# A two-block conditioned transformer on one core: x normalised on ScalarE in attention, attention's stages reordered, and setup cut at another place

## The chip, the cores and the metric

One core of one Trainium2 chip runs one program. The metric is its device time in microseconds (us), the median of several executions. The engines are named as in the profile: PE is TensorE's matmul and PEld its weight load, DVE VectorE, ACT ScalarE, POOL GpSimd, SP SyncE. A name with a q (SPq, ACTq) is the engine's queue, which issues DMAs.

## What is computed

x is (128, 64, 256) in f32: 128 sequences of 64 rows and 256 channels; cond is (128, 256), one row per sequence. The first block, cut to its core:

```
ada = silu(cond) @ ada_w.T + ada_b        # 6 rows of 256 per sequence: gamma1,2 scale1,2 shift1,2
x1  = ln(x) * (scale1 + 1) + shift1
q, k, v = split(x1 @ mat_qkv_w.T + bias)  # 16 heads of 16
q = l2norm(q) * exp(scale_mul);  k = l2norm(k)
o   = softmax(q @ k.T) @ v
x   = x + (o @ proj_w.T + proj_b) * gamma1
x2  = ln(x) * (scale2 + 1) + shift2
x   = x + (gelu(x2 @ fc1_w.T + fc1_b) @ fc2_w.T + fc2_b) * gamma2
```

The second block is linear attention with a modulation of its own, `silu(cond) @ emb_W + emb_b` (the third modulation here), and a last product.

## The kernel before

The program has four parts, each a block of instructions for all engines, with a barrier of all engines between them: setup (L187), attention_pass (L444), feed_forward_pass and linear_pass. x stays in SBUF as x_all, 64 tiles of two sequences (128 rows) in 16 groups of four. The change touches setup and attention_pass.

*Setup.* SyncE's queue loads cond, proj_w, ada_w (1.5 MB), the first group of x (512 KB), the qkv weights (768 KB) and emb_w (512 KB), waits for the gammas, stores them to DRAM and loads three more groups of x. PE multiplies the activated cond: first with the gamma columns (512 wide, L349), then 16 products with 2*C and more (scale and shift 1 and 2, L354), then 8 for the third modulation (L361). VectorE adds the biases (L398 to L418). Every f32 weight is split in a high and a low bf16 half: ScalarE makes the high one (L289, L291), POOL subtracts (L322, L324).

*Attention.* Five engines run the tiles as a software pipeline. Each engine has a list of stages with a lag: at step n it does, in the list's order, each stage of tile n - lag. So the order in the list is the order of the instructions on that engine, and everything across engines is a semaphore wait. The first 16 steps are written out, the middle is a loop over four steps, the last steps are written out again. `reuse(eng, sem, t, slots)` waits until a buffer of `slots` copies is free.

```
pipeline(sp, [(9, load_gain), (5, place_v), (5, place_k), (0, load_later)])
pipeline(pool, [(5, normalise), (1, rstd_of), (12, add), (2, x1_low), (8, e_lo), (0, split_fc)])
```

A tile goes so: statistics and aggregate on DVE (mean, variance), rstd_of on POOL, hat on DVE (L916: x_hat = (x - mean) * rstd, 128x256), turn_x on PE (two transposes into ps_x), modulate on DVE and modulate_second on ACT (x1_t), x1_high on ACT and x1_low on POOL (x_split), qkv on PE (six products of 512 columns into ps_qk, L809, and six of 256 into ps_v, L816), biases on DVE, v_hi on ACT and v_low on DVE, square on ACT, reduce_norms on DVE (L837, L839), logs and factor on ACT, normalise on POOL (qk_hat, L630), turn_qk on PE (L800), qk_hi on ACT (L710), qk_lo on DVE (L908). place_v and place_k on SyncE copy v and k into block form inside SBUF, for two tiles at a time: at odd tiles, four DMAs into v_pairs (L608) and eight into k_pairs (L593). place_v waits for pv_done of the tile four before, which frees the buffer; place_k for qk_lo. Then scores on PE (48 small products, L790, waits for the eight k copies), high_exponentials and full_exponentials on ACT (L725, L730), e_lo on POOL (L657, 128x1024), probs_v on PE (L775, signals pv_done), outputs on DVE, turn_o on PE (L764), o_hi on ACT, o_low on DVE, project on PE (L751, L754), residual on DVE, add on POOL. ps_y of project and ps_v of qkv share a bank, as do ps_x's halves for turn_x and turn_o; bank_free waits keep them apart. load_gain loads the rows of gamma1 from DRAM for two tiles. load_later loads the other 12 groups of x and the fc weights; split_fc splits these at tiles 7 and 14 (ACT) and one later (POOL, 128x2048).

Of the kernel before, what the change touches and what calls it, by code (L numbers as in the profile page):

```python
# [109 lines left out]


class Shared:


    def __init__(self, nc, ctx):
# [5 lines left out]
        self.minus_half = sb("minus_half", [P, UNROLL], F32)  # L121
        self.eps_norm3 = sb("eps_norm3", [P, 1], F32)
# [64 lines left out]
def setup(nc, m, x, cond, qkv_w, q_bias, scale_mul, proj_w, proj_b, ada_w, ada_b, fc2_b,  # L187
          emb_w, out_b, columns):

    with ExitStack() as ctx:  # L190
# [8 lines left out]
        cond_t = sb("cond_t", [P, NC_, B])  # L199
        w_ada = sb("w_ada", [P, NC_, 6 * C])  # L200
        w_emb = sb("w_emb", [P, NC_, 2 * C])
        b_ada_row = sb("b_ada_row", [P, 2 * C])
        b_ada, b_emb, g_sn, b_sn = m.b_ada, m.b_emb, m.g_sn, m.b_sn
        gamma_rows = sb("gamma_rows", [P, 2 * C])
# [3 lines left out]
        scale_plus = sb("scale_plus", [P, NC_, B])  # L208
        b_sn_half = sb("b_sn_half", [P, NC_])
# [8 lines left out]
        ps = [ctx.enter_context(nc.psum_tensor(f"set_ps{i}", [P, 512], F32)) for i in range(6)]  # L218
# [4 lines left out]
        emb_here = sem("emb_here")  # L223
# [14 lines left out]
        b_halved = sem("b_halved")  # L238
# [5 lines left out]
        modulations = sem("modulations")  # L244
        gammas_made = sem("gammas_made")
        gammas_stored = sem("gammas_stored")
# [10 lines left out]
        def _(sp):  # L257
            load(sp, [(cond_sb[:], cond)], cond_here)
            load(sp, [(proj_full[:], proj_w.rearrange(CHUNKED, p=P))], proj_here)
            load(sp, [(w_ada[:], ada_w.rearrange(CHUNKED, p=P))], ada_here)  # L260
            load(sp, [(m.x_all[:, X_PARTS[0]:X_PARTS[1]], x_tiles(x)[:, X_PARTS[0]:X_PARTS[1]])], m.x_here[0])
            load(sp, [(qkv_full[:], qkv_w.rearrange(CHUNKED, p=P))], qkv_here)
            load(sp, [(w_emb[:], emb_w.rearrange(CHUNKED, p=P))], emb_here)
            sp.wait_ge(gammas_made, 1)
            sp.dma_start(m.gammas, gamma_rows[:]).then_inc(gammas_stored, 16)
            sp.wait_ge(gammas_stored, 16)
            part = slice(X_PARTS[1], X_PARTS[2])
            load(sp, [(m.x_all[:, part], x_tiles(x)[:, part])], m.x_here[1])
            sp.wait_ge(attention_here, 16)

        @block.scalar
        def _(act):
# [8 lines left out]
            load(act, [(m.b_fc2[:], row(fc2_b))], m.ff_here)  # L281
# [5 lines left out]
            act.activation(m.norm_weight[:, 0:H], head_scale[:], ACT.Exp, scale=-2.0)  # L287
            act.wait_ge(qkv_here, 16)
            act.activation(m.w_qkv[:, HI], qkv_full[:], ACT.Copy).then_inc(qkv_hi_made, 1)  # L289
            act.wait_ge(proj_here, 16)  # L290
            act.activation(m.w_proj[:, HI], proj_full[:], ACT.Copy).then_inc(proj_hi_made, 1)  # L291

        @block.gpsimd
        def _(pool):
# [6 lines left out]
            pool.memset(m.eps_ln[:], 1e-6).then_inc(consts_made, 1)  # L301
            pool.memset(m.same_head[:], 1.0).then_inc(consts_made, 1)
# [16 lines left out]
            pool.memset(m.v_split[:, :, :, HI, :, 2 * HD:], 1.0)  # L319
            pool.wait_ge(rows_cleared, 2)  # L320
            pool.wait_ge(qkv_hi_made, 1)
            pool.tensor_tensor(m.w_qkv[:, LO], qkv_full[:], m.w_qkv[:, HI], ALU.subtract)  # L322
            pool.wait_ge(proj_hi_made, 1)
# [1472 lines left out]
```

## Time and profile before

| | us |
|---|---|
| median of 3 runs | 1266.47 |
| lowest, highest | 1264.91, 1266.75 |
| the profiled execution, its own time | 1262.96 |
| its span, first to last instruction | 1261.2 |
| setup | 0 to 24.5 |
| attention | 24.5 to about 495 |

| engine | busy us | share |
|---|---|---|
| PE | 1128.5 | 89% |
| PEld | 818.5 | 65% |
| DVE | 960.6 | 76% |
| ACT | 795.3 | 63% |
| POOL | 848.9 | 67% |

Busy time counts neither waits nor the issue of DMAs. The shares are means over parts with different limits, so the order of work in attention has to be read from timelines. In a timeline, several instructions of a group are drawn together (x48), and the bracket at the end gives the idle time of the engine before the first of them, and what released it. TensorE's loads of weights (PEld) start with their products and overlap them.

### The profile page before, as it was taken

The page shows a single profiled execution, that of the slowest core. Times are in us where ns is not written, and L with a number is a line of the kernel's source. Part 1 is how long each engine was busy: PE and PEld are TensorE (multiplying, and loading weights), DVE is VectorE, ACT ScalarE, POOL GpSimd, SP SyncE. Part 2 cuts the span into 40 slices and gives each one's busy share as a digit, 9 for nine tenths or more (in the row PEclk, how much of TensorE's full clock was granted, in tenths as well). Part 3 has the DMA queues.
Part 4 walks back from the last instruction along what each step waited for, and adds up shares of the span by engine and source line. Part 5 has one row for each costly group of instructions (what it writes and reads, how often), then busy time and mean ns, then how long its engine had stood idle before and what let it go on. Part 6 is the DMA issues. An engine that isn't in the chain of part 4 may idle for free. (4 is left out here: it accounts for less than half of the span.)

```text
span 1261.2 us, 37486 instructions
## 1 busy us (share of the span) xinstructions
PE 1128.5 (89%) x11946; PEld 818.5 (65%) x12098; DVE 960.6 (76%) x2338; ACT 795.3 (63%) x2141; POOL 848.9 (67%) x1018
## 2 busy tenths in 40 slices
PE   4687999999999975699999999997899999999997
PEld 3476677777777764366666676765566666766664
DVE  6687999999999963755655555543899999999985
ACT  2676787887787862445544545441677777777774
POOL 4667777777777754537675667563367777777777
PEclk9898999999999998699999999998999999999999
DMA  7552222222222221200101010100011111111112
GB/s 265 145 147 52 63 55 60 61 57 59 62 57 59 62 54 32 76 18 18 34 17 33 17 33 17 34 18 17 6 28 56 42 40 56 42 54 42 39 57 81
DMA packets 138945, 68.13 MB, mean 54 GB/s; under 512 B 76544, under 2 KB 137600, under 8 KB 138880
## 3 DMA queue, kind: packets, MB, share of 16 engines
q1 hardware_dynamic: 110480, 41.32, 13.1%
q10 hardware_dynamic: 28400, 25.99, 7.2%
q8 instruction: 35, 0.57, 0.2%
q14 instruction: 30, 0.25, 0.1%
HBM read 41.58 MB, written 8.65 MB: 40 GB/s over the span
## 5 line engine op out<-in xcount | busy, mean ns | idle before, releaser
L1128 PE MATMUL f_ps_y<-w_fc,f_h_split 128*128 128x256 bf16 x1536 | 172.7, 273 | 1.4 <-DVE f_branch L1247 1.4
L1155 PE MATMUL f_ps_h<-f_x_split,w_fc 128*128 128x512 bf16 x737 | 166.4, 383 | 4.3 <-DVE f_biases L1278 1.4
L1128 PEld LDWEIGHTS f_ps_y<-w_fc,f_h_split 128*128 128x128 bf16 x1536 | 150.2, 98 | 22.5 <-issue 1.7
L657 POOL TENSOR_TENSOR e_split<-e_full,e_split 128x1024 bf16<-128x1024 f32 x64 | 136.5, 2133 | 39.7 <-ACT e_full L730 39.7
L1255 DVE TENSOR_TENSOR f_h_split<-f_h,f_h_split 128x512 bf16<-128x512 f32 x64 | 64.0, 1002 | 104.3 <-ACT f_h L1114 104.2
L1489 ACT ACTIVATE l_z_t<-l_ps_yt,shift,scale 128x64 f32<-128x64 f32 x256 | 82.6, 402 | 92.3 <-PE l_ps_yt L1555 56.2
L1155 PEld LDWEIGHTS f_ps_h<-f_x_split,w_fc 128*128 128x128 bf16 x768 | 75.6, 99 | 88.7 <-issue 3.3
L1113 ACT ACTIVATE f_h_split<-f_ps_h,columns 128x512 bf16<-128x512 f32 x128 | 89.1, 696 | 66.5 <-POOL f_h_split L1074 36.2
L790 PE MATMUL ps_s<-qk_t,k_pairs 128*128 128x64 bf16 x3072 | 102.6, 195 | 29.0 <-DMA k_pairs<-qk_t 25.4
L790 PEld LDWEIGHTS ps_s<-qk_t,k_pairs 128*128 128x128 bf16 x3072 | 97.9, 99 | 37.3 <-issue 19.0
L1074 POOL TENSOR_TENSOR f_h_split<-f_h,f_h_split 128x512 bf16<-128x512 f32 x64 | 79.7, 1255 | 36.6 <-ACT f_h L1114 36.6
L637 POOL TENSOR_TENSOR x_split<-x_t,x_split 128x256 bf16<-128x256 f32 x64 | 42.9, 671 | 84.0 <-ACT x_split L678 84.0
L1606 PE MATMUL l_ps_qv<-w_qvk,l_x_split 128*128 128x512 bf16 x324 | 82.3, 383 | 13.9 <-issue 6.6
L1101 ACT ACTIVATE f_x_split<-f_x 128x1024 bf16<-128x1024 f32 x16 | 16.9, 1057 | 118.9 <-POOL f_x L1041 118.9
L1114 ACT ACTIVATE f_h<-f_ps_h,columns 128x512 f32<-128x512 f32 x128 | 89.6, 700 | 0.0
L809 PE MATMUL ps_qk<-w_qkv,x_split 128*128 128x512 bf16 x323 | 83.3, 390 | 4.3 <-POOL x_split L637 0.8
L725 ACT ACTIVATE e_split<-ps_s,minus_shift 128x1024 bf16<-128x1024 f32 x64 | 71.2, 1112 | 21.2 <-PE ps_s L790 21.1
L1458 POOL TENSOR_TENSOR l_rstd<-l_mean_var,eps_norm 128x2 f32<-128x2 f32 (+1 forms) x73 | 14.1, 194 | 101.5 <-DVE l_mean_var L1649 76.2
L1520 ACT ACTIVATE l_kq<-l_ps_k,l_k_tops 128x64 f32<-128x64 f32 x256 | 77.9, 341 | 1.1 <-DVE l_k_tops L1684 0.9
L730 ACT ACTIVATE e_full<-ps_s,minus_shift 128x1024 f32<-128x1024 f32 x64 | 70.8, 1106 | 0.0
L630 POOL TENSOR_TENSOR qk_hat<-qk,factors 128x512 f32<-128x512 f32 x64 | 67.7, 1058 | 1.5 <-ACT factors L703 1.5
L1041 POOL TENSOR_TENSOR f_x<-f_x,shift 128x1024 f32<-128x1024 f32 x16 | 31.0, 1940 | 53.7 <-DVE f_x L1187 53.7
(180 smaller groups left out, 3152.5 us busy)
## 6 DMA issues: line engine op xcount, KB each, us to landing
v_pairs<-v_split SPq DMA_DIRECT2D x128, 66.0 KB, 2.1
k_pairs<-qk_t SPq DMA_DIRECT2D x256, 32.0 KB, 2.2
gain<-gammas SPq DMA_DIRECT2D x64, 128.0 KB, 3.1
f_gain<-gammas ACTq DMA_DIRECT2D x32, 256.0 KB, 4.3
l_gate<-in_cond ACTq DMA_DIRECT2D x128, 64.0 KB, 2.6
out<-x_all ACTq DMA_DIRECT2D x16, 512.0 KB, 2.9
x_all<-in_x SPq DMA_DIRECT2D x13, 512.0 KB, 5.6
fc_full<-in_L_cond_fc_w SPq DMA_DIRECT2D x2, 1024.0 KB, 7.5
```

What stands on the lines that cost most here:

```text
L657: pool.tensor_tensor(flat(e_split[a][:, LO]), flat(e_full[:]), flat(e_split[a][:, HI]), ALU.subtract).then_inc(e_lo_made, 1)
L725: act.activation(flat(e_split[a][:, HI]), flat(ps_s[:]), ACT.Exp, bias=m.minus_shift[:])
L790: last = pe.matmul(ps_s[:, s, G_ * c + g], k_pairs[:, t.slot(4), k, c, s, g].rearrange("p r k -> p (r k)"), qk_t[:, 0, t.slot(4), q, c, s ...
L809: last = pe.matmul(ps_qk[:, :], x1_split[a][:, xs, c, :], m.w_qkv[:, ws, c, 0:2 * C], start=(i == 0 and c == 0), stop=(i == 2 and c == NC_ ...
L1074: pool.tensor_tensor(h_split[a][:, LO, f], h[f % 4][:], h_split[a][:, HI, f], ALU.subtract).then_inc(h_lo_odd, 1)
L1113: act.activation(h_split[a][:, HI, f], ps_h[f % 4][:], ACT.Gelu, bias=m.b_fc1[:, f:f + 1])
L1114: act.activation(h[f % 4][:], ps_h[f % 4][:], ACT.Gelu, bias=m.b_fc1[:, f:f + 1]).then_inc(h_made, 1)
L1128: last = pe.matmul(ps_y[:, i], h_split[a][:, hs, f, i * P:(i + 1) * P], m.w_fc2[:, ws, f], start=(f == 0 and k == 0), stop=(f == F_CHUNKS ...
L1155: last = pe.matmul(ps_h[f % 4][:], m.w_fc1[:, ws, c, f * P:(f + 1) * P], x2_split[a][:, xs, c], start=(k == 0 and c == 0), stop=(k == 2 an ...
L1489: act.activation(z_t[a][:, c, s * L:(s + 1) * L], ps_yt[:, c, s * L:(s + 1) * L], ACT.Identity, bias=by_seq(m.shift3, c, t, s), scale=by_s ...
L1520: act.activation(kq[t.slot(4)][:, i * L:(i + 1) * L], ps_k[:, c, s * L:(s + 1) * L], ACT.Exp, bias=k_tops[a][:, c, s:s + 1], scale=-1.0, a ...
L1606: last = pe.matmul(ps_qv[:], x3_split[a][:, xs, c], m.w_qvk3[:, ws, c, 0:2 * C], start=(i == 0 and c == 0), stop=(i == 2 and c == NC_ - 1))
```

## The change

In attention:

- The five lists are reordered, as below. hat moves from DVE to ACT and becomes an activation with scale rstd and bias centre = -mean * rstd; POOL makes centre in two more operations on 128x1, each behind a wait. statistics keeps its lag, rstd_of goes from lag 1 to 0, hat from 1 to 0, normalise on POOL from 5 to 4, place_v and place_k from 5 to 6.
- load_gain's wait for branch_made now also stands in the loop.
- The third modulation's products are made by PE in step 0 (into ps_s), its eight VectorE operations in steps 1 and 2 (four each, the last in the list). The first scores wait for them, as does SyncE's load of the fc1 weights at tile 3, since the tiles they use now lie in that buffer. fc2_b is loaded by SyncE in step 0.

In setup:

- SyncE loads the qkv weights ahead of x, and the three later groups of x before it waits for the gammas; it no longer waits for their store.
- PE makes the 16 products for scales and shifts first, then the gammas.
- k_pairs is cleared by VectorE for three quarters, later in its order, and by POOL for one. ACT splits proj_w first, then the qkv weights. VectorE, not POOL, makes the low half of proj_w. POOL's low half of the qkv weights comes last.

```diff
             load(sp, [(w_ada[:], ada_w.rearrange(CHUNKED, p=P))], ada_here)
+            load(sp, [(qkv_full[:], qkv_w.rearrange(CHUNKED, p=P))], qkv_here)
             load(sp, [(m.x_all[:, X_PARTS[0]:X_PARTS[1]], x_tiles(x)[:, X_PARTS[0]:X_PARTS[1]])], m.x_here[0])
-            load(sp, [(qkv_full[:], qkv_w.rearrange(CHUNKED, p=P))], qkv_here)
-            load(sp, [(w_emb[:], emb_w.rearrange(CHUNKED, p=P))], emb_here)
-            sp.wait_ge(gammas_made, 1)
-            sp.dma_start(m.gammas, gamma_rows[:]).then_inc(gammas_stored, 16)
-            sp.wait_ge(gammas_stored, 16)
+            load(sp, [(m.w_emb, emb_w.rearrange(CHUNKED, p=P))], m.emb_here)
             part = slice(X_PARTS[1], X_PARTS[2])
             load(sp, [(m.x_all[:, part], x_tiles(x)[:, part])], m.x_here[1])
+            sp.wait_ge(gammas_made, 1)
+            sp.dma_start(m.gammas, m.gamma_rows).then_inc(m.gammas_stored, 16)
...
+            pool.memset(m.k_pairs[:, 3], 0.0)
...
-            pool.tensor_tensor(m.w_proj[:, LO], proj_full[:], m.w_proj[:, HI], ALU.subtract)
...
+            dve.tensor_tensor(m.w_proj[:, LO], proj_full[:], m.w_proj[:, HI], ALU.subtract)
...
             def load_gain(t):
-                if isinstance(t.n, int):
-                    reuse(sp, branch_made, t, 4)
+                reuse(sp, branch_made, t, 4)
...
                 if isinstance(t.n, int) and t.n == FC1_AT:
+                    sp.wait_ge(m.gammas_stored, 16)
+                    sp.wait_ge(modulations3_made, NC_)
...
-            pipeline(sp, [(9, load_gain), (5, place_v), (5, place_k), (0, load_later)])
+            pipeline(sp, [(6, place_v), (6, place_k), (0, load_later), (9, load_gain)])
...
+                pool.wait_ge(rstd_made, t.n + 1)
+                pool.tensor_tensor(centre[t.slot(4)][:], mean_var[t.slot(4)][:, 0:1], rstd[t.slot(4)][:], ALU.mult
+                                   ).then_inc(mean_scaled, 1)
+                pool.wait_ge(mean_scaled, t.n + 1)
+                pool.tensor_tensor(centre[t.slot(4)][:], centre[t.slot(4)][:], m.minus_one[:], ALU.mult
+                                   ).then_inc(centre_made, 1)
...
-            pipeline(pool, [(5, normalise), (1, rstd_of), (12, add), (2, x1_low), (8, e_lo), (0, split_fc)])
+            pipeline(pool, [(12, add), (0, split_fc), (0, rstd_of), (2, x1_low), (8, e_lo), (4, normalise)])
...
+            def hat(t):
+                a = t.slot(2)
+                act.wait_ge(centre_made, t.n + 1)
+                reuse(act, x_hat_t, t, 2)
+                act.activation(x_hat[a][:, None, :], t.rows(m.x_all), ACT.Identity, bias=centre[t.slot(4)][:],
+                               scale=rstd[t.slot(4)][:]).then_inc(x_hat_made, 1)
...
-            pipeline(act, [(4, v_hi), (4, square), (2, modulate_second), (8, high_exponentials), (5, qk_hi),
-                           (10, o_hi), (2, x1_high), (8, full_exponentials), (4, logs), (0, split_fc),
-                           (4, factor)])
+            pipeline(act, [(2, modulate_second), (4, v_hi), (4, square), (2, x1_high), (8, high_exponentials),
+                           (10, o_hi), (4, logs), (5, qk_hi), (8, full_exponentials), (4, factor), (0, split_fc),
+                           (0, hat)])
...
+            def emb_products(t):
...
             def scores(t):
                 a = t.slot(2)
+                if isinstance(t.n, int) and t.n == 0:
+                    pe.wait_ge(modulations3_made, NC_)
...
-            pipeline(pe, [(8, scores), (11, project), (5, turn_qk), (9, probs_v), (10, turn_o), (3, qkv), (1, turn_x)])
+            pipeline(pe, [(8, scores), (9, probs_v), (10, turn_o), (5, turn_qk), (11, project), (1, turn_x),
+                          (3, qkv), (0, emb_products)])
...
+            def modulation3(t):
...
-            pipeline(dve, [(4, biases), (2, modulate), (4, v_low), (10, outputs), (4, reduce_norms),
-                           (11, residual), (10, o_low), (1, hat), (5, qk_lo), (-1, statistics), (0, aggregate)])
+            pipeline(dve, [(2, modulate), (4, biases), (10, outputs), (-1, statistics), (4, v_low), (0, aggregate),
+                           (4, reduce_norms), (10, o_low), (5, qk_lo), (11, residual), (0, modulation3)])
```

What this makes of PE's order in one step of attention, before, from the scores (ps_s) to turn_x:

```order
L790 MATMUL ps_s<-qk_t,k_pairs 128x64 x48
L751 MATMUL ps_v<-bias_rows,ones 128x256
L754 MATMUL ps_v<-w_proj,o_t 128x256 x6
L800 MATMUL ps_qkt<-ident,qk_hat 128x128 x4
L775 MATMUL ps_o<-v_pairs,e_split 128x66 x24
L764 MATMUL ps_x<-ident,o_full 128x128 x2
L809 MATMUL ps_qk<-w_qkv,x_split 128x512 x6
L816 MATMUL ps_v<-w_qkv,x_split 128x256 x6
L826 MATMUL ps_x<-ident,x_hat 128x128 x2
```

and the same step of PE with the change:

```order
L803 MATMUL ps_s<-qk_t,k_pairs 128x64 x48
L776 MATMUL ps_o<-v_pairs,e_split 128x66 x24
L765 MATMUL ps_x<-ident,o_full 128x128 x2
L813 MATMUL ps_qkt<-ident,qk_hat 128x128 x4
L752 MATMUL ps_v<-bias_rows,ones 128x256
L755 MATMUL ps_v<-w_proj,o_t 128x256 x6
L839 MATMUL ps_x<-ident,x_hat 128x128 x2
L822 MATMUL ps_qk<-w_qkv,x_split 128x512 x6
L829 MATMUL ps_v<-w_qkv,x_split 128x256 x6
```

probs_v (ps_o) and turn_o stand directly behind the scores; project went from second to behind turn_qk, and turn_x ahead of qkv.

ACT's order in one step, before, with the semaphores that each waits for:

```order
L690 ACTIVATE v_split<-ps_v 128x2x4x32 [waits v_pairs_here0,qkv_done]
L684 ACTIVATE squares<-qk 128x512 [waits norms_made,qk_biased]
L670 ACTIVATE x_t<-ps_x,shift,scale 128x64 [waits x1_lo_made,x1_made]
L670 ACTIVATE x_t<-ps_x,shift,scale 128x64
L725 ACTIVATE e_split<-ps_s,minus_shift 128x1024 [waits pv_done,scores_done]
L710 ACTIVATE qk_t<-ps_qkt 128x2x256 [waits scores_done,qk_turned]
L736 ACTIVATE o_t<-ps_x 128x256 [waits proj_done,o_turned]
L678 ACTIVATE x_split<-x_t 128x256 [waits qkv_done,x1_second]
L730 ACTIVATE e_full<-ps_s,minus_shift 128x1024 [waits e_lo_made]
L696 ACTIVATE log_norms<-norms 128x32 [waits factors_made,norms_weighted]
L703 ACTIVATE factors<-log_norms,log 128x32 [waits qk_hat_made,logs_made]
```

and with the change:

```order
L664 ACTIVATE x_t<-ps_x,shift,scale 128x64 [waits x1_lo_made,x1_made]
L664 ACTIVATE x_t<-ps_x,shift,scale 128x64
L691 ACTIVATE v_split<-ps_v 128x2x4x32 [waits v_pairs_here0,qkv_done]
L685 ACTIVATE squares<-qk 128x512 [waits norms_made,qk_biased]
L679 ACTIVATE x_split<-x_t 128x256 [waits qkv_done,x1_second]
L726 ACTIVATE e_split<-ps_s,minus_shift 128x1024 [waits pv_done,scores_done]
L737 ACTIVATE o_t<-ps_x 128x256 [waits proj_done,o_turned]
L697 ACTIVATE log_norms<-norms 128x32 [waits factors_made,norms_weighted]
L711 ACTIVATE qk_t<-ps_qkt 128x2x256 [waits scores_done,qk_turned]
L731 ACTIVATE e_full<-ps_s,minus_shift 128x1024 [waits e_lo_made]
L704 ACTIVATE factors<-log_norms,log 128x32 [waits qk_hat_made,logs_made]
L672 ACTIVATE x_hat<-x_all,centre,rstd 128x256 [waits x_hat_t,centre_made]
```

x1_high (x_split) now comes ahead of the high exponentials, logs ahead of qk_hi and of the full exponentials, and x_hat stands last.

## Rows read from the trace of the kernel before

**Rows 1.** Attention, one stretch: busy us of PE, PEld, DVE, ACT, POOL; clock, DMA share
```profile
180.00:240.00 60.00, 55.61 (x871) 42.73 (x878) 56.02 (x134) 47.74 (x99) 46.34 (x54) 1.00 0.27 59
```

**Rows 2.** Timeline of PEld, one pair of steps: start, us, line, tiles
```profile
209.77 1.46 PEld L790 LDWEIGHTS ps_s<-qk_t,k_pairs 128*128 128x128 bf16 x48 [0.49 <-issue]
211.40 0.10 PEld L751 LDWEIGHTS ps_v<-bias_rows,ones 128*128 128x128 bf16 x1 [0.17 <-issue]
...
212.16 0.42 PEld L800 LDWEIGHTS ps_qkt<-ident,qk_hat 128*128 128x128 f32 x4
212.55 0.89 PEld L775 LDWEIGHTS ps_o<-v_pairs,e_split 128*128 128x128 bf16 x24
...
213.54 1.07 PEld L809 LDWEIGHTS ps_qk<-w_qkv,x_split 128*128 128x128 bf16 x6
...
215.74 0.20 PEld L826 LDWEIGHTS ps_x<-ident,x_hat 128*128 128x128 f32 x2 [0.26 <-issue]
215.91 1.55 PEld L790 LDWEIGHTS ps_s<-qk_t,k_pairs 128*128 128x128 bf16 x48
...
223.18 0.40 PEld L790 LDWEIGHTS ps_s<-qk_t,k_pairs 128*128 128x128 bf16 x12 [0.66 <-issue]
```

**Rows 3.** SyncE's queue beside it, and its wait for probs_v in the whole run
```profile
213.59 2.60 SPq L608 DMA_DIRECT2D v_pairs<-v_split  x4
216.32 5.24 SPq L593 DMA_DIRECT2D k_pairs<-qk_t  x8
...
SPq L608 <- PE ps_o L775: 90.8, 24, 8.4
```

**Rows 4.** Waits from 60 to 450 us: in total, times, longest
```profile
PE ps_s L790 <- DMA k_pairs<-qk_t: 12.5, 26, 1.6
```

**Rows 5.** Groups from 60 to 450 us: busy us, mean ns, idle before
```profile
L916 DVE TENSOR_SCALAR x_hat<-x_all,mean_var,rstd 128x256 f32 (+1 forms) x56 | 46.8, 836 | 5.8 <-POOL rstd L624 5.8
...
L670 ACT ACTIVATE x_t<-ps_x,shift,scale 128x64 f32<-128x64 f32 x112 | 39.1, 399 | 1.4 <-DVE x_t L849 0.2
...
L839 DVE SCALAR_TENSOR_TENSOR norms<-norms,norm_weight 128x32 f32<-128x32 f32 x56 | 31.0, 553 | 1.9
...
L678 ACT ACTIVATE x_split<-x_t 128x256 bf16<-128x256 f32 x57 | 23.2, 408 | 0.0
...
L622 POOL TENSOR_TENSOR rstd<-mean_var,eps_ln 128x1 f32<-128x1 f32 x56 | 10.7, 191 | 0.0
```

**Rows 6.** The tile ps_s in the whole run; ACT and POOL in that pair
```profile
L790 PE MATMUL ps_s<-qk_t,k_pairs x3072: 189/193/242, 51.0 to 489.9; 128*128 128x64 bf16 x192
...
212.94 0.60 ACT L710 ACTIVATE qk_t<-ps_qkt 128x512 bf16<-128x512 f32 x1
...
214.44 1.11 ACT L730 ACTIVATE e_full<-ps_s,minus_shift 128x1024 f32<-128x1024 f32 x1
...
215.62 2.13 POOL L657 TENSOR_TENSOR e_split<-e_full,e_split 128x1024 bf16<-128x1024 f32 x1 [0.25 <-ACT e_full L730]
```

**Rows 7.** Setup and the first tiles: the first 35 us, and rows of the timeline
```profile
0.00:35.00 35.00, 17.11 (x77) 11.53 (x79) 22.05 (x49) 9.54 (x16) 16.05 (x34) 0.86 0.82 277
...
11.87 3.50 PE L349 MATMUL set_ps<-w_ada,cond_t 128*128 128x512 f32 x4
...
15.21 3.73 PE L354 MATMUL set_ps<-cond_t,w_ada 128*128 128x128 f32 x32
...
16.28 1.48 ACT L289 ACTIVATE w_qkv<-qkv_full 128x1536 bf16<-128x1536 f32 x1 [5.89 <-DMA qkv_full<-in_L_cond_mat_qkv_w]
...
22.08 0.34 DVE L410 TENSOR_SCALAR scale_plus<-set_ps,columns 128x128 f32<-128x128 f32 x1
...
24.54 0.89 DVE L895 BATCH_NORM_STATS2 stats<-x_all 128x6 f32<-128x256 f32 x2 [0.30 <-PEq L190]
...
26.44 0.41 DVE L916 TENSOR_SCALAR x_hat<-x_all,mean_var,rstd 128x256 f32<-128x256 f32 x1 [0.94 <-POOL rstd L624]
...
36.26 0.19 DVE L839 SCALAR_TENSOR_TENSOR norms<-norms,norm_weight 128x32 f32<-128x32 f32 x1
```

More of the change, by code:

```diff
@@ L346, in _ @@
             pe.wait_ge(ada_here, 16 * 2)
-            for c in range(NC_):
-                last = pe.matmul(ps[1][:, :], cond_t[:, c, :], w_ada[:, c, 0:2 * C], start=(c == 0), stop=(c == NC_ - 1))
-            last.then_inc(products, 1)
             for k in range(8):
@@ L357, in _ @@
             last.then_inc(products, 1)
-            pe.wait_ge(emb_here, 16)
-            for k in range(4):
-                for c in range(NC_):
-                    last = pe.matmul(ps[4][:, k * B:(k + 1) * B], w_emb[:, c, k * P:(k + 1) * P], cond_t[:, c, :],
-                                     start=(c == 0), stop=(c == NC_ - 1))
+            for c in range(NC_):
+                last = pe.matmul(ps[1][:, :], cond_t[:, c, :], w_ada[:, c, 0:2 * C], start=(c == 0), stop=(c == NC_ - 1))
             last.then_inc(products, 1)
@@ L780, in probs_v @@
                 last.then_inc(pv_done, 1)
+            def emb_products(t):
+                if isinstance(t.n, int) and t.n == EMB_AT:
+                    pe.wait_ge(m.emb_here, 16)
+                    for k in range(4):
+                        for c in range(NC_):
+                            last = pe.matmul(flat(ps_s[:])[:, k * B:(k + 1) * B], m.w_emb[:, c, k * P:(k + 1) * P],
+                                             m.cond_t[:, c, :], start=(c == 0), stop=(c == NC_ - 1))
+                    last.then_inc(emb_done, 1)
             def scores(t):
                 a = t.slot(2)
+                if isinstance(t.n, int) and t.n == 0:
+                    pe.wait_ge(modulations3_made, NC_)
                 pe.wait_ge(k_pairs_here[t.u // 2], (t.j + 1) * 16 * HPC)
@@ L910, in qk_lo @@
                                   qk_t[:, :, t.slot(4), HI].rearrange("p w c k -> p w (c k)"), ALU.subtract).then_inc(qk_lo_made, 1)
-            def hat(t):
-                a = t.slot(2)
-                dve.wait_ge(rstd_made, t.n + 1)
-                reuse(dve, x_hat_t, t, 2)
-                dve.tensor_scalar(x_hat[a][:, None, :], t.rows(m.x_all), mean_var[t.slot(4)][:, 0:1], rstd[t.slot(4)][:],
-                                  ALU.subtract, ALU.mult).then_inc(x_hat_made, 1)
             def biases(t):
```

93 lines of the change are left out of this document (50 added, 43 removed).

## The prediction

> **What bounds the kernel now.** I read the busy times of one stretch of the attention loop first, then the timeline of TensorE's weight loads, since it shows where the stages of a tile begin, then SyncE's queue beside it, and the waits last. From 180 to 240 us PE is busy 55.6 of 60 us and DVE 56.0 [rows 1]; both look like the bound, and neither is it alone. The starts of the scores tell more: 209.77, 215.91, 223.18 [rows 2]. The steps alternate, 6.14 and 7.27 us, and only the pair, 13.41, repeats. At the end of the long step PE waits for the DMA of k_pairs: 26 such waits in the 57 tiles from 60 to 450 us [rows 4], one in nearly every pair. SyncE copies k and v of two tiles at a time, in order on one queue. At 213.59, right behind probs_v of that step (its loads begin at 212.55), it issues four copies of v, at 216.32 eight copies of k, and the scores that need them begin at 223.18 [rows 2, 3]. SyncE's waits for that product sum to 90.8 us [rows 3], so it is the product that releases it. The ring is: scores to v 3.82, v to k 2.73, k to the next scores 6.86; 13.41 in all, exactly the pair. While this ring stands, less work on any engine gives nothing. In its first leg PE does project (from 211.40) and turn_qk (from 212.16) between the scores and probs_v [rows 2].
>
> **What stands next under it.** 60 us hold 8.95 tiles of 6.705. Busy per tile: DVE 6.26, ACT 5.33, POOL 5.18, PE 6.21 [rows 1]. PE's ends overlap its next starts. Taken from start to start, without waits, its stages need 1.46 for the scores, 0.76 project, 0.39 turn_qk, 0.99 probs_v with turn_o, 1.94 qkv (2.20 less the 0.26 idle), 0.17 turn_x: 5.71 [rows 2].
>
> **The change, part by part.**
>
> *PE's order.* probs_v and turn_o now stand directly behind the scores. The leg from scores to v becomes 1.46 + 1.04 (212.55 to 213.59) = 2.50 instead of 3.82 [rows 2, 3]. The ring is 2.50 + 2.73 + 6.86 = 12.09, or 6.05 a tile. This has two conditions. First, probs_v must find the low half of e_split. I lay out one step from the start of its scores, with durations from [rows 5, 6]: scores done 1.6, high exponential until 2.75 (as long as the full one), o_hi until 3.2 (turn_o ends near 2.7), logs until 3.35, qk_hi until 3.9, full exponential until 5.0 (1.11), POOL's low half until 7.2 (2.13). The next probs_v comes 1.46 behind the next scores, at 7.65 with 6.2 a tile: 0.45 to spare. Before, the full exponential began 4.67 behind the scores (214.44 against 209.77) [rows 2, 6], now at 3.9, because x1_high is done ahead of it. Second, k must be ready when v has been issued, at 5.2; qk_lo follows qk_hi and ends near 4.7: 0.5 to spare.
>
> *SyncE's order.* place_v and place_k move one step later in the list, gain behind them; but this queue is paced by its waits, and the sequence is still v, k, gain. v and k take 2.60 + 5.24 = 7.84 us of a pair [rows 3], so there is room for gain's two copies in 12. Their new wait is for branch_made of a tile whose residual comes right behind the qk_lo that k waited for, so it has passed before k's 5.24 us of issue are over. Cost nothing; if that residual came 5 us late, v and the ring would be late with it. The load of fc2 now goes ahead of a k, once.
>
> *x_hat to ScalarE.* VectorE loses 0.84 a tile [rows 5] and comes to 5.42. ScalarE gains one activation of 128x256 f32 out of SBUF. It has no such row; the nearest is x_split's 0.41, the far end two of x_t's 0.40 with scale and bias, 0.80 [rows 5]. I take 0.41, nearest in size: ScalarE 5.74. POOL gets two operations on 128x1 like rstd's first, 0.19 [rows 5], each with a handover of 0.08: 0.54 in all, POOL 5.72. POOL is idle 13.7 of 60 us now, 1.5 a tile [rows 1], which covers it; without that cover x_split's low half and the exponentials' would come 0.5 later. The chain to x_hat is longer by 0.54, but rstd_of and hat run a step ahead of turn_x, with about 3 us to spare. The Trainium skill speaks against this move: "ScalarE: Activation LUTs", Rules for kernel authors, keeps multiply and add on VectorE, and its budget of about 0.3 us plus 0.83 ns an element makes 0.51 us, an estimate. Were that 0.1 more on the path at every tile, the forecast below would be 1237. The trace does not bear out the preference here: VectorE takes 0.41 for x_hat when alone [rows 7], but 0.84 on average beside POOL.
>
> *VectorE's order.* Its starts now add up to about 5.6 a tile, but it hands over to ScalarE once a round: norms, then logs and qk_hi on ScalarE, then qk_lo, residual, modulate, biases, outputs, stats, v_low, norms. That ring is 5.6 less o_low's 0.35 plus 0.8 on ScalarE: 6.05. On PE, turn_x now waits some 0.1 for o_low, and the v product 0.1 for residual, so PE needs about 5.9.
>
> So four rings lie between 5.9 and 6.05 a tile. The bounds are 5.9 (PE alone) and 6.70 (as now). I take 6.2, near the rings with a little for their meeting at different phases: a pair of 12.4 against 13.41, 0.505 a tile. From the first scores (51.0) to the last (489.9) there are 63 steps [rows 6], the late part of the fill and the drain included, where PE waits for k too: **-31.8 us**. The two long steps in which the fc weights are split stay as they are.
>
> *Setup.* VectorE's last eight operations, for the third modulation, run from 22.08, and attention begins at 24.54 [rows 7]. They are gone from here. The qkv weights come ahead of x's first 512 KB, which at 277 GB/s take 1.9 us [rows 7]: ScalarE's split begins near 14.4 instead of 16.28 and takes 1.5, and POOL's subtraction follows it as before, near 16 to 19.2, with the three operations that stood behind it put ahead or on VectorE. PE makes those for scales and shifts first (3.7 us), then gammas (3.5) [rows 7]; from 11.0, a little earlier than 11.87, they end near 18.5. VectorE adds gammas (0.7) and w_proj's low half (0.7): 20.0. Both ways end near 20: **-4.0 us**, with bounds of -2 (loads hold it) and -5.
>
> *Fill.* The eight operations come back in steps 1 and 2 (2.2 us, half of them in VectorE's idle time); PE's eight products for them lie beside the statistics; the first x_hat comes 0.5 later. VectorE without x_hat gives back 0.3 a step for four steps. **+0.5 us**, bounds -1 and +2.5.
>
> Sum: -31.8 - 4.0 + 0.5 = -35.3. The profiled execution took 1262.96 us, so 1227.7; it lies 3.5 below the median of the three runs, 1266.47, which gives **1231**.
>
> **Rivals.**
>
> *Half the gain.* The near rings meet badly and a tile takes 6.5. For it: my layout already has a wait of 0.1 on PE at two places and spares of 0.5. Against: the present loop holds its ring to 0.1 us. 0.2 x 63 = 13, with setup 16: 1250. Chance 0.16.
>
> *VectorE's hindrance goes too.* The norms' last operation averages 0.55 [rows 5] and took 0.19 in the fill with POOL idle [rows 7]; in the new order it falls beside POOL's small operations. VectorE's ring shortens by 0.35, and PE's 5.9 binds: 0.8 x 63 = 50, with setup 54: 1212. Against: k's ring of 6.05 would have to shorten as well. Chance 0.08. "SBUF — State Buffer" in the Trainium skill says of the port pair that VectorE and GpSimd share that whichever starts first keeps it for its whole instruction; these two rows agree.
>
> *No gain in the loop.* probs_v starts 2.8 behind the scores as it does now, since the low half comes 1.8 later than laid out. Setup alone: 1263. Chance 0.08, half of it within 0.2%.
>
> *Slower.* On ScalarE logs now stands ahead of qk_hi and of the full exponential, and waits for VectorE's norms, which stand behind outputs, stats and v_low. From the start of logs to the end of the low half it is 4.0 us; probs_v is second in PE's step, and all else of the step queues behind it. So a tile costs (start of logs) + 4.0 - 1.46. I put logs at 3.2; from 4.2 on a tile is 6.74 and the change loses. At 4.5 it is 7.04: 0.33 x 63 = 21, less setup 3.5: 1284. For it: VectorE has the least idle time. Against: it has just lost 0.84 a tile. Chance 0.06.
>
> **Numbers.** My own case has 0.62. The range 1214 to 1250 takes in my bounds, the half gain and most of the second rival; outside are the last two rivals and tails. A measurement of this kernel can tell 0.2%, 2.5 us, from no change. Faster: 0.62 + 0.16 + 0.08 + a third of the third, 0.89; same 0.05; slower 0.06.
>
> **What would show it.** The first statistics near 20.4. Scores of every second tile 12.4 apart, v issued 2.5 behind them. x_hat on ScalarE at 0.41 to 0.45. VectorE under 90% busy in the loop. It is wrong if PE's largest wait in the loop is probs_v's for POOL's e_split (no gain, or slower), or if the pair stays 13.4 with scores waiting for k_pairs: then v did not move with probs_v.

## The result and the profile after

| | before | after |
|---|---|---|
| median of 4 runs each, us | 1265.69 | 1224.89 |
| lowest, highest | 1263.74, 1266.75 | 1223.19, 1225.94 |
| ratio, 95% interval | | 0.9683 (0.9666 to 0.9701) |
| profiled execution, its span | 1262.96, 1261.2 | 1224.19, 1222.3 |
| first statistics | 24.54 | 25.57 |
| first scores, last scores | 50.98, 488.56 | 57.99, 446.40 |
| last scores to the end of the span | 772.6 | 775.9 |

The change takes 40.8 us off; forecast were 35.3. The sum of the profiled executions is +1.0 (setup), +6.0 (first statistics to first scores), -49.2 (first to last scores), +3.3 (behind them): -38.9. None of my three terms had its size: setup and fill came out 5.0 and 5.5 worse than forecast, the loop 17.4 better, and the 3.3 at the end weren't in the forecast. That the sum came out near the forecast is in part luck: these errors have opposite signs.

The same stretch of 60 us of the loop as in [rows 1], after:

```profile
180.00:240.00 60.00, 58.60 (x982) 48.34 (x990) 53.66 (x141) 56.13 (x121) 55.34 (x81) 1.00 0.36 66
```

TensorE has gone from 55.61 to 58.60 of 60, VectorE down from 56.02 to 53.66, ScalarE and GpSimd up by 8.4 and 9.0, since they do more tiles and new work. TensorE's timeline of one pair of steps, after (start, us, line; L755 is project):

```profile
210.94 1.57 PE L803 MATMUL ps_s<-qk_t,k_pairs 128*128 128x64 bf16 x48 [0.23 <-DMA k_pairs<-qk_t]
212.35 0.91 PE L776 MATMUL ps_o<-v_pairs,e_split 128*128 128x66 bf16 x24
213.10 0.41 PE L765 MATMUL ps_x<-ident,o_full 128*128 128x128 f32 x2
213.35 0.60 PE L813 MATMUL ps_qkt<-ident,qk_hat 128*128 128x128 f32 x4
...
213.89 0.82 PE L755 MATMUL ps_v<-w_proj,o_t 128*128 128x256 bf16 x6
...
216.85 1.56 PE L803 MATMUL ps_s<-qk_t,k_pairs 128*128 128x64 bf16 x48
...
222.97 0.70 PE L803 MATMUL ps_s<-qk_t,k_pairs 128*128 128x64 bf16 x18
```

SyncE's queue beside it, to be read against [rows 3]:

```profile
209.78 1.50 SPq L551 DMA_DIRECT2D gain<-gammas  x2
213.29 2.61 SPq L596 DMA_DIRECT2D v_pairs<-v_split  x4
216.01 5.24 SPq L581 DMA_DIRECT2D k_pairs<-qk_t  x8
221.51 1.50 SPq L551 DMA_DIRECT2D gain<-gammas  x2
225.32 2.61 SPq L596 DMA_DIRECT2D v_pairs<-v_split  x4
```

Scores to v 2.35, v to k 2.72, k to the next scores 6.96: 12.03 us, one pair, against 13.41. The ring is the one of the prediction, its first leg shorter. Its last leg now ends with TensorE nearly full: the wait for k, 0.23 here, is all that is left of it.

### The profile page after: what moved, and what is told of

Same layout as the page of the kernel before. It is cut to its first block and busy times, and to the rows that moved or that the text cites. A ratio compares the mean times of both kernels' runs of the same rounds, so it can differ in the third digit from the quotient of the medians.

```text
span 1222.3 us, 37712 instructions
## 1 busy us (share of the span) xinstructions
PE 1111.3 (91%) x11946; PEld 819.8 (67%) x12098; DVE 917.5 (75%) x2275; ACT 814.2 (67%) x2205; POOL 874.1 (72%) x1147
## 5 line engine op out<-in xcount | busy, mean ns | idle before, releaser
L1570 PE MATMUL l_ps_out<-w_out,l_silu 128*128 128x256 f32 x256 | 65.9, 380 | 0.0
```

The source lines that it names most:

```text
L1570: last = pe.matmul(ps_out[:], silu[a][:, c], m.w_out3[:, c], start=False, stop=(c == NC_ - 1))
```

## The experiments

The kernel before, measured again beside each of these runs, took 1263.1 to 1264.8 us, and beside the changed kernel 1265.7. The ratios are to that; "off" and "slower" are differences of medians from 1224.89, and by the ratios they come out up to 3 us otherwise. So differences of that size are read from the traces.

**One list alone, in both directions.** In the kernel before, TensorE does probs_v and turn_o directly behind the scores (turn_x stays last, unlike in the change); in the changed kernel, project and turn_qk come between the scores and probs_v again, as before:

```diff
-            pipeline(pe, [(8, scores), (11, project), (5, turn_qk), (9, probs_v), (10, turn_o), (3, qkv), (1, turn_x)])
+            pipeline(pe, [(8, scores), (9, probs_v), (10, turn_o), (11, project), (5, turn_qk), (3, qkv), (1, turn_x)])
```

> The kernel before with one edit: TensorE's list alone is put in the new order at its head (scores, probabilities times v, turn_o, project, turn_qk, qkv, turn_x). Theory of the ring: the way from the scores to v's transfers falls from 3.82 to about 2.5 us, so the ring falls from 13.41 to about 12.1 us a pair; but VectorE still has x_hat and its own 6.26 us a tile, so that the pair can't be under 12.6: 12.6 to 12.8 us a pair, 0.35 us a tile times 63 = 22 us off, 1244 us (1238 to 1252). Rival, that moving x_hat to ScalarE is what paid and the list is beside the point: the pair stays near 13.4 us, 1262 to 1268 us.

```diff
-            pipeline(pe, [(8, scores), (9, probs_v), (10, turn_o), (5, turn_qk), (11, project), (1, turn_x),
+            pipeline(pe, [(8, scores), (11, project), (5, turn_qk), (9, probs_v), (10, turn_o), (1, turn_x),
```

> The changed kernel with one edit: TensorE does project and turn_qk between the scores and probabilities times v again, as before. Theory of the ring: from scores to v's transfers 3.8 us again, 1.3 to 1.5 us more a pair, which is 0.7 us a tile: pair 13.3 to 13.5 us, about 63 x 0.7 = 44 us slower, 1262 to 1272 us. Rival (x_hat's move and the new lists of the other engines paid): at most 10 us slower, 1225 to 1235 us.

Measured: 1338.0 (ratio 1.0585, 1.0567 to 1.0603) and 1324.6 (1.0482, 1.0464 to 1.0499). Both theories missed both runs, by 52 us and more. TensorE in the first of them, one step:

```profile
208.39 1.56 PE L790 MATMUL ps_s<-qk_t,k_pairs 128*128 128x64 bf16 x48
211.51 0.91 PE L775 MATMUL ps_o<-v_pairs,e_split 128*128 128x66 bf16 x24 [1.56 <-DVE o_full L874]
...
216.21 0.43 PE L826 MATMUL ps_x<-ident,x_hat 128*128 128x128 f32 x2 [0.39 <-DVE x_hat L916]
```

probs_v, which used to come late, overwrites the bank that VectorE's outputs of the tile before reads, and these stand behind modulate in VectorE's list, which waits for turn_x, which waits for x_hat near the list's end. A round of VectorE's list now hangs in TensorE's, and each step lasts 8.2 us in place of 6.7. In the second run turn_x waits about 1.0 for o_low and project 0.7 to 0.9 for v_low, and a step is 7.94 on average:

```profile
208.47 0.28 PE L752 MATMUL ps_v<-bias_rows,ones 128*128 128x256 bf16 x1 [0.70 <-DVE v_split L894]
...
211.78 0.44 PE L839 MATMUL ps_x<-ident,x_hat 128*128 128x128 f32 x2 [0.93 <-DVE o_t L913]
```

So the lists of the four engines are one order of work. The shorter leg is worth having only with outputs early on VectorE and the exponentials early on ScalarE, and these runs, rather than test the ring, put another in its place. The gain of TensorE's list can't be told apart from those reorderings, and no run takes back VectorE's, ScalarE's or SyncE's list alone.

**The ring, tested by its length.** The same bytes of v in one issue more; nothing else moves:

```diff
                 for s in range(SEQ):
                     for r in range(2):
-                        sp.dma_start(
+                        for tt in ((slice(t.u - 1, t.u), slice(t.u, t.u + 1)) if s == 0 and r == 0 else (two,)):
+                            sp.dma_start(
```

> The changed kernel with one of the four transfers of v's pair issued as two of half the size: the same bytes, one issue more, 0.65 us by the 5.24 us of eight. Theory of the ring: each pair is 0.65 us longer, 12.67 us, and 0.33 x 63 = 20 us more, 1245 us (1238 to 1248). Rival (the loop is bound by TensorE, SyncE's issues have slack of 1 us a pair or more): within 3 us of 1224.9.

Measured: 1245.19 (ratio 0.9833, 0.9812 to 0.9854), 20.3 above the changed kernel, as the first theory had it.

```profile
199.68 3.14 SPq L597 DMA_DIRECT2D v_pairs<-v_split  x5
202.94 5.23 SPq L581 DMA_DIRECT2D k_pairs<-qk_t  x8
208.42 1.51 SPq L551 DMA_DIRECT2D gain<-gammas  x2
212.22 3.13 SPq L597 DMA_DIRECT2D v_pairs<-v_split  x5
```

The five take 3.14 in place of 2.61, and the pair is 12.54 in place of 12.03: what SyncE needs more, the pair is longer. This is the run that shows the ring, and that SyncE has no slack although its issues fill 9.4 of 12 us. The size fits less well than the time: one issue more costs 0.53, not the 0.65 taken, and 0.26 a tile makes 16 us over the 63 steps. Between first and last scores the run is 23.0 us longer in its profiled execution; the other 7 lie in the early and the last steps.

**The ring, shortened.** k ahead of v; then three of v's transfers ahead of k and one behind:

```diff
-            pipeline(sp, [(6, place_v), (6, place_k), (0, load_later), (9, load_gain)])
+            pipeline(sp, [(6, place_k), (6, place_v), (0, load_later), (9, load_gain)])
```

> The changed kernel with one edit: SyncE issues a pair's eight transfers of k before the four of v. Theory of the ring (scores, probabilities times v, v's transfers, k's transfers, scores of the pair after): v's 2.7 us leave it and k waits for qk_lo instead, some 4.4 us behind the scores, so that it is 4.4 + 6.95 = 11.35 us a pair, and TensorE at some 5.75 us a tile (58.60 busy of 60.00 now) takes over the bound: a pair of 11.5 to 11.7 us, 0.2 us a tile times 63 = 12 us off, 1213 us (1208 to 1219). Rival (TensorE's own work bounds the loop already, the wait for k is slack that it would lose elsewhere): the pair stays at 12.0, within 3 us of 1224.9.

```diff
-            pipeline(sp, [(6, place_v), (6, place_k), (0, load_later), (9, load_gain)])
+            pipeline(sp, [(6, place_v), (6, place_k), (6, place_v_last), (0, load_later), (9, load_gain)])
```

> The changed kernel with three of v's four transfers ahead of k's eight and the fourth behind them. Theory: the ring that closed anew with all of v behind k (v late, then v_hi, qk_lo, k) stays open, since the fourth transfer is issued by 10 us behind the scores and is there about when v_hi of the step after next wants it; the ring through the scores is 0.6 us shorter (k starts at qk_lo's end, 215.4 in place of 216.01), so that TensorE's own work of 5.86 us a tile bounds: 11.72 a pair, 0.3 us less, 9 us off, 1216 us (1214 to 1221). Rival: v_hi waits up to 0.8 us for the fourth transfer and that comes back by qk_lo and k: 1222 to 1240 us.

Measured: 1266.21 (1.0008, 0.9996 to 1.0020) for k first, which is the whole gain gone. Its waits from 150 to 400 us (in total, times, longest):

```profile
ACT v_split L691 <- DMA v_pairs<-v_split: 31.1, 19, 2.3
...
PE ps_x L839 <- DVE o_t L913: 21.8, 19, 1.2
```

The old ring is open: TensorE's waits for k sum to 0.2 us there. A new one took its place: v is issued behind k, v_hi waits 1.6 us a pair for the old v to have been copied out, and v_hi stands second in ScalarE's list, so that logs, qk_hi, qk_lo and the next k come late. SyncE's queue, and v_hi between:

```profile
196.46 5.26 SPq L581 DMA_DIRECT2D k_pairs<-qk_t  x8
201.84 2.60 SPq L596 DMA_DIRECT2D v_pairs<-v_split  x4
...
209.74 5.26 SPq L581 DMA_DIRECT2D k_pairs<-qk_t  x8
```

```profile
205.89 0.39 ACT L691 ACTIVATE v_split<-ps_v 128x256 bf16<-128x256 f32 x1 [1.58 <-DMA v_pairs<-v_split]
```

k to v 5.38, v to v_hi 4.05, v_hi to k 3.85: 13.28, the pair. I had looked at who waits for k and not at who waits for v.

Three and one: 1219.04 (0.9634, 0.9621 to 0.9647), 5.9 off, within the expected range, but not by the expected way. TensorE's wait for k is gone from the list, and four steps still sum to 24.04 us (6.14, 6.05, 6.05, 5.80; 24.02 before the edit). What is left over the stretch from 150 to 400 us:

```profile
DVE qk_t L940 <- ACT qk_t L713: 14.2, 41, 0.5
POOL e_split L653 <- ACT e_full L733: 7.7, 21, 0.4
ACT x_t L666 <- DVE x_t L881: 7.4, 21, 0.4
```

So behind k's ring another round, through ScalarE and its handovers to VectorE and GpSimd, has the same length within 0.05 us a pair. The gain in the profiled execution, 3.5 of span, came at the ends: 2.0 less from first to last scores, in their early and late steps, 2.3 less behind them, 0.8 more ahead. Two later runs say where the other round runs. With qk_hi ahead of logs on ScalarE and v as in the change, four steps are still 24.0; with qk_hi ahead and v in three and one (the last run, under "Together"; its third edit, the clearing, leaves the loop at 12.0 a pair when alone) they are 23.8, and VectorE's waits for qk_hi over the same stretch fall from 14.2 us to 7.2. So both rounds stood at 12.0, and the second goes through logs and qk_hi.

**x_hat back on VectorE**, at the end of its list, without GpSimd's two operations for the centre:

```diff
-                           (10, o_hi), (4, logs), (5, qk_hi), (8, full_exponentials), (4, factor), (0, split_fc),
-                           (0, hat)])
+                           (10, o_hi), (4, logs), (5, qk_hi), (8, full_exponentials), (4, factor), (0, split_fc)])
...
+            def hat(t):
+                a = t.slot(2)
+                dve.wait_ge(rstd_made, t.n + 1)
+                reuse(dve, x_hat_t, t, 2)
+                dve.tensor_scalar(x_hat[a][:, None, :], t.rows(m.x_all), mean_var[t.slot(4)][:, 0:1], rstd[t.slot(4)][:],
+                                  ALU.subtract, ALU.mult).then_inc(x_hat_made, 1)
...
-                           (4, reduce_norms), (10, o_low), (5, qk_lo), (11, residual), (0, modulation3)])
+                           (4, reduce_norms), (10, o_low), (5, qk_lo), (11, residual), (0, hat), (0, modulation3)])
```

> The changed kernel with x_hat back on VectorE (mean subtracted and rstd multiplied in one instruction, last of its list), GpSimd's two small operations for the centre left out. VectorE then has some 5.6 + 0.3 to 0.45 us of work a tile, under 6.01. Theory of the ring: the pair stays within 0.2 us of 12.03, -3 to +6 us in all, 1222 to 1231 us. Rival (VectorE had to be relieved for the pair to fall): pair 12.6 or more, 18 us or more slower, 1243 us or more.

Measured: 1230.70 (0.9736, 0.9720 to 0.9752), at the top of the first theory's range. The steps are 6.19 and 6.08 in turn, 12.27 a pair, 0.24 above 12.03 where at most 0.2 was expected. Its groups on VectorE and GpSimd, 180 to 240 us:

```profile
L932 DVE TENSOR_SCALAR x_hat<-x_all,mean_var,rstd 128x256 f32 x9 | 3.6, 404 | 0.0
```

```profile
L645 POOL TENSOR_TENSOR e_split<-e_full,e_split 128x1024 bf16<-128x1024 f32 x10 | 22.7, 2273 | 7.4 <-ACT e_full L718 7.4
```

x_hat takes 0.404 here and took 0.836 in [rows 5], on the same engine. It isn't alone here: GpSimd's e_lo runs beside it. What differs is who starts first. VectorE and GpSimd before the change, then in this run:

```profile
214.70 0.82 DVE L916 TENSOR_SCALAR x_hat<-x_all,mean_var,rstd 128x256 f32 x1
```

```profile
214.70 0.67 POOL L637 TENSOR_TENSOR x_split<-x_t,x_split 128x256 bf16<-128x256 f32 x1 [1.12 <-ACT x_split L678]
```

```profile
209.46 0.40 DVE L932 TENSOR_SCALAR x_hat<-x_all,mean_var,rstd 128x256 f32 x1
```

```profile
209.57 2.29 POOL L645 TENSOR_TENSOR e_split<-e_full,e_split 128x1024 bf16<-128x1024 f32 x1 [0.69 <-ACT e_full L718]
```

Before, 55 of the 56 x_hat from 60 to 450 us start together with x1_low or up to 0.1 us ahead of it, and each ends 0.15 us behind x1_low's end. Here 52 of 56 start 0.1 to 0.2 us ahead of e_lo and keep 0.40, while e_lo takes 2.27 in place of 2.13; three have nothing beside them and take 0.405. In the one that starts behind e_lo, x_hat takes 1.36 and ends, again, 0.15 behind it. So half of x_hat's time on VectorE was waiting for a GpSimd operation. The move to ScalarE is worth 6 or 7 of the 41 us against this placing on VectorE.

**The setup.** k_pairs cleared on VectorE ahead of all else, as before:

```diff
         def _(dve):
+            dve.memset(m.k_pairs[:], 0.0)
...
-            dve.memset(m.k_pairs[:, 0:3], 0.0)
...
-            pool.memset(m.k_pairs[:, 3], 0.0)
```

> The changed kernel with k_pairs cleared wholly on VectorE ahead of everything, as before, and no part of it on GpSimd. Theory: the setup came out late because VectorE's first copies and its memset stood beside GpSimd's memsets and ahead of the chain of the biases; with the memset done by about 8 us the first statistics come at 20.5 to 22.5 us instead of 25.57: 3 to 5 us off, 1220 to 1222 us. Rival (the order of the weights' splits and the loads set that time): the first statistics stay within 1 us of 25.57 and the time within 1.5 us of 1224.9.

Measured: 1221.47 (0.9665, 0.9648 to 0.9682), 3.4 off, or 2.3 by the ratios, whose intervals overlap (the changed kernel has 0.9666 to 0.9701). The trace is clearer: first statistics at 20.5, and the profiled execution's span 3.1 shorter. The changed kernel's GpSimd, then its VectorE, from 3.5 us on:

```profile
3.54 3.62 POOL L316 MEMSET v_pairs<- 128x4224 bf16 x1
...
7.22 3.81 POOL L319 MEMSET k_pairs<- 128x4096 bf16 x1
```

```profile
5.43 1.87 DVE L363 COPY b_v_wide<-columns 128x256 f32<-128x256 f32 x1
7.23 3.83 DVE L365 TENSOR_SCALAR head_scale<-head_scale 128x16 f32<-128x16 f32 x1
12.41 5.18 DVE L367 MEMSET k_pairs<- 128x6144 uint32 x1 [1.35 <-issue]
17.50 0.11 DVE L370 TENSOR_REDUCE top<-head_exp 128x1 f32<-128x16 f32 x1
```

And VectorE with the edit:

```profile
2.59 6.88 DVE L358 MEMSET k_pairs<- 128x8192 uint32 x1 [2.59 <-issue]
9.39 0.36 DVE L360 COPY fc_full<-set_ps 128x256 f32<-128x256 f32 x1
9.67 0.28 DVE L363 COPY b_v_wide<-columns 128x256 f32<-128x256 f32 x1
9.86 0.17 DVE L365 TENSOR_SCALAR head_scale<-head_scale 128x16 f32<-128x16 f32 x1
10.39 0.17 DVE L369 TENSOR_REDUCE top<-head_exp 128x1 f32<-128x16 f32 x1 [0.36 <-ACT head_exp L282]
```

An operation on 128x16 lasts 3.83 us beside a clearing of 3.81 on GpSimd, and 0.17 alone; it ends when the clearing ends. Then comes VectorE's own 5.18 us. The chain of the biases starts at 17.5 instead of 10.4. Cleared first, while VectorE has nothing else, it costs less, though not nothing: the first copy comes at 9.39 in place of 5.09, and TensorE's 16 products, which need it, at 11.87 in place of 10.47. By the port pair of "SBUF — State Buffer" in the Trainium skill whichever engine starts first keeps it for its whole instruction, and the rows agree. (x_hat's rows above agree but for starts less than 0.1 us apart, where VectorE waited although its recorded start is the earlier.) Of the 5.0 us that the start gained, 0.3 went again in the fill and 1.9 between first and last scores, where one early step became 9.87 us long.

**The fill.** Three tries. The third modulation's products and what follows them moved later; qk_hi ahead of logs; with that, x1_low ahead of rstd_of:

```diff
-    EMB_AT, FC1_AT, FC1_SPLIT, FC2_AT, FC2_SPLIT = 0, 3, 7, 10, 14
+    EMB_AT, FC1_AT, FC1_SPLIT, FC2_AT, FC2_SPLIT = 4, 6, 9, 11, 14
```

> The changed kernel with the third modulation's products in step 4 in place of step 0, fc1's load in step 6 (3 before), its split in steps 9 and 10 (7 and 8), fc2's load in step 11 (10). Theory: the products of 3.75 us at the low clock and VectorE's wait of 2.21 us for them stand at the head of attention, where nothing else is in the lists to cover them, and fc1's 6 us split stands ahead of the first scores: first scores 2.5 to 5 us sooner (53 to 55.5 us in place of 57.99), all of it kept, 1220 to 1222 us. Rival (the fill is bound by the chain through VectorE's list from step 1 on and the work just moves): first scores within 1 us of 57.99 and the time within 1.5 us.

```diff
-                           (10, o_hi), (4, logs), (5, qk_hi), (8, full_exponentials), (4, factor), (0, split_fc),
+                           (10, o_hi), (5, qk_hi), (4, logs), (8, full_exponentials), (4, factor), (0, split_fc),
```

> The changed kernel with qk_hi ahead of logs in ScalarE's list. Theory: a step of the fill lasts 4.45 us because qk_lo on VectorE waits 0.78 us for qk_hi, which stands behind logs, which waits 0.68 us for the norms; with qk_hi first a step of the fill lasts some 3.7 us, first scores 3 to 4.5 us sooner, the loop unchanged at 12.0 us a pair: 1220.5 to 1222 us. Rival (the fill is bound by TensorE and the normalise chain, turn_qk's wait of 1.5 us): first scores within 1 us, time within 1.5 us of 1224.9; or slower, where the factors come later in the loop by this: up to 5 us.

```diff
-            pipeline(pool, [(12, add), (0, split_fc), (0, rstd_of), (2, x1_low), (8, e_lo), (4, normalise)])
+            pipeline(pool, [(12, add), (0, split_fc), (2, x1_low), (0, rstd_of), (8, e_lo), (4, normalise)])
```

> The changed kernel with qk_hi ahead of logs (ScalarE, as in the run before) and, new, x1_low ahead of rstd_of in GpSimd's list. Theory: in the fill VectorE's modulate waits 0.70 us a step for x1_low, which stands behind the four small operations for rstd and centre; with x1_low first a step of the fill lasts 3.7 us in place of 4.37, first scores at 53 to 55.5 us in place of 57.29, the loop the same or up to 0.1 us a tile either way: 1217 to 1219 us. Rival (turn_qk's wait of 1.50 for qk_hat or x_hat, now later, closes the step as well): first scores at 56.5 us or later, 1219.5 to 1223 us.

Products later: 1234.58 (0.9769, 0.9751 to 0.9787), 9.7 slower, both theories wrong. The first turn_x starts at 28.66 without them and at 29.11 with them, so they cost next to nothing in step 0. But SyncE's load of fc1 waits for the modulation, and SyncE's queue is in order:

```profile
52.30 0.37 SPq L562 DMA_DIRECT2D fc_full<-in_L_cond_fc_w  x1
52.72 0.47 SPq L566 DMA_DIRECT2D x_all<-in_x  x1
53.24 2.71 SPq L596 DMA_DIRECT2D v_pairs<-v_split  x4
55.99 5.30 SPq L581 DMA_DIRECT2D k_pairs<-qk_t  x8
```

v stood at 44.09 and k at 51.01 in the changed kernel. First scores came at 62.99, 5.0 later, and another 5.7 went between first and last scores, in the early steps.

qk_hi first: 1220.64 (0.9673, 0.9644 to 0.9702; one of the four runs took 1229.4), 4.3 off by the medians, 1.3 by the ratios, whose intervals overlap; in the profiled executions 4.8. The time fell in the expected range, but not by the expected way: first scores came only 0.7 sooner, at 57.29, and of the rest 2.1 lie between first and last scores, the loop still at 12.02 a pair, and 2.0 behind the last, unexplained. A step of the fill still lasts 4.37 us. Its VectorE row tells why:

```profile
46.60 0.59 DVE L879 TENSOR_SCALAR x_t<-ps_x,scale,shift 128x64 f32<-128x64 f32 x2 [0.71 <-POOL x_split L631]
```

The wait for qk_hi gave way to one for x1_low, which stands on GpSimd behind rstd and the two new operations for the centre (44.53 to 45.83). The wall behind the wall was 0.08 us away.

x1_low first as well: 1227.47 (0.9711, 0.9696 to 0.9726). The step of the fill stayed at 4.38, now with x_hat waiting for the centre, and the loop became slower, 12.13 a pair:

```profile
L869 DVE SCALAR_TENSOR_TENSOR norms<-norms,norm_weight 128x32 f32<-128x32 f32 x10 | 4.6, 459 | 0.3
```

The norms' last operation takes 0.459 in place of 0.192, since x1_low now starts ahead of it on GpSimd; one of them, with GpSimd's row:

```profile
219.75 0.64 DVE L869 SCALAR_TENSOR_TENSOR norms<-norms,norm_weight 128x32 f32<-128x32 f32 x1
```

```profile
219.68 0.67 POOL L631 TENSOR_TENSOR x_split<-x_t,x_split 128x256 bf16<-128x256 f32 x1
```

It ends 0.05 behind x1_low's end. In the changed kernel GpSimd's small operations for rstd (128x1) lie beside it, and it takes 0.192 all the same. Both expectations missed this.

**Together.** Clearing, qk_hi and x1_low; then clearing, qk_hi and v in three and one:

> Together: k_pairs cleared on VectorE at its head, qk_hi ahead of logs, x1_low ahead of rstd_of. If the parts add (3.4 and 4.3 us measured alone, 2 us expected of x1_low): 1214 to 1217 us, first scores near 49 to 51 us. Rival (what the start gains is given back at the step of the fourth pair of tiles, as 1.9 us of 4.8 were with the clearing alone): 1217.5 to 1221 us.

> The changed kernel with the three edits that each made it faster alone: k_pairs cleared on VectorE at its head (1221.5), qk_hi ahead of logs (1220.6), three of v's transfers ahead of k's and one behind (1219.0). If they add to 1224.9: 1211 us (1209 to 1214). Rival (they overlap: each one's gain lay in the same fill and drain, the loop keeps its 12.0 us a pair): 1215 to 1219 us.

Measured: 1222.95 (0.9668, 0.9655 to 0.9681), above both its ranges, since x1_low's edit costs more than taken, and **1213.83** (0.9586, 0.9567 to 0.9605), just inside the first theory's. The second is the fastest of all, 11.1 below the changed kernel by the medians. The three edits alone give 3.4, 4.3 and 5.9, 13.6 in sum, so four fifths of it add; by the ratios they give 2.3, 1.3 and 6.2, 9.8 in sum, against 12.3 together. So they add by and large, and how far can't be told more closely. The loop:

```profile
180.00:240.00 60.00, 59.70 (x1011) 49.59 (x1008) 53.90 (x142) 56.81 (x123) 56.00 (x81) 1.00 0.36 68
```

Four steps are now 23.81 us (6.11, 5.83, 6.03, 5.84), 11.9 a pair, at a granted clock of 1.00, the 2.4 GHz level. First scores come at 52.32, and the fill from the first statistics on is 31.6 us, as good as unchanged. With TensorE busy 59.70 of 60, what is next to be shortened is most likely its own work; that wasn't tried.

## Why the prediction was right in its sum and not in its parts

- **The ring and the new order: right.** I said that scores, v, k and scores again bound the loop, that the first leg would be 2.50 (2.35) and the ring 12.09 (12.03), and the run with one issue more shows it for the changed kernel; for the kernel before it rests on the trace, where the legs sum to the pair. The layout of a step held: full exponential at 3.9 (3.64 measured), e_lo done at 7.2 (7.05).
- **Loop, -31.8 against -49.2: mis-sized.** The step "I take 6.2, near the rings with a little for their meeting at different phases" failed: the rounds met without loss, 6.01 a tile. 0.19 x 63 = 12. Another 2 are the step before: I had 6.705 from one pair, and the 40 steps from the 15th on average 6.74. The other 3 lie in the early steps and the drain, which I had priced like the middle: the early pairs were 8.0 to 8.4 + 5.8 long, and are 6.6 to 7.4 + 5.8.
- **x_hat, 0.41: the wrong row.** Measured:

```profile
L672 ACT ACTIVATE x_hat<-x_all,centre,rstd 128x256 f32 (+1 forms) x57 | 33.9, 595 | 0.0
```

  0.595, midway between my ends; x_split's row has the size but neither scale nor bias read from memory; that these are the cause, no run here shows. The estimate by "ScalarE: Activation LUTs" in the Trainium skill, 0.51, was nearer and still short; that budget is for one operand read from memory (the bias), and x_hat has two. The page's preference for VectorE is half borne out: 0.404 there, if it starts ahead of GpSimd's long operation. ScalarE had the room. GpSimd's two operations take 0.19 each, as taken.
- **VectorE's hindrance, a rival at 0.08: half of it happened.** The norms' operation fell from 0.553 [rows 5] to 0.192 in the loop as that rival said: before, GpSimd's add had started ahead of it, and in the new order rstd's small operations lie there. It did not become 1212: k's ring stood at 12.03, the reason given against it, and so did the round through logs and qk_hi.
- **SyncE's order, "cost nothing": right** in the loop.
- **Setup, -4.0 against +1.0: the step failed.** I followed the loads and the weights' splits and left out an edit that was in the diff: the clearing of k_pairs, moved behind VectorE's first copies and partly to GpSimd. "Both ways end near 20" took VectorE's chain as free. With the clearing put back the first statistics come at 20.5, the forecast 20.4.
- **Fill, +0.5 against +6.0: outside its bounds.** "VectorE without x_hat gives back 0.3 a step" was wrong. A step of the fill became a round over four engines of 4.45 us. The two walls found (logs ahead of qk_hi; the centre ahead of x1_low) are worth little apart, and what would undo the 6 us isn't found.
- The 3.3 us behind the last scores: not explained. TensorE's first work of the feed-forward comes 23.6 behind them, 21.1 before.

## What to carry to other kernels

When engines run fixed lists, reorder them together: one list alone cost 75 and 100 us here where the whole gave 41. After a ring is found, ask for each transfer in it who waits for its end, not only for the one that is late; k first undid the gain by v's reader. Look for operations of VectorE that take longer than when alone, and place them so that no long operation of GpSimd (here 0.67 us and more) has started just ahead, and clear large buffers before the chain starts, not inside it; and check every moved line of a diff, a clearing too.

## What the hardware did that I had not expected

- A clearing on GpSimd (write only, bf16) holds up VectorE as much as an operation with inputs does: 0.17 became 3.83, 0.28 became 1.87.
- A long operation of GpSimd that starts first, or less than 0.1 us later, held two of VectorE's operations until it ended: x_hat ended 0.15 us behind it (0.82 to 1.36 in place of 0.40), the norms' operation 0.05 behind it (0.64 beside x1_low in place of 0.19). The small ones on 128x1 didn't lengthen the norms' operation: 0.192 beside them. Where VectorE started 0.1 us or more ahead, GpSimd paid: e_lo 2.27 in place of 2.13.
- SyncE's time to issue goes by the number of transfers more than by their bytes: four took 2.61, five with the same bytes 3.14.
